# 24 of 84 weight blocks are prepared by GpSimd in the mixer of a decoder layer, and attention keeps 15 a batch

## The reference, cut to what matters

```python
# 1 mixer: project to 128 channels, two gated state-space layers over the 4 sequences' transposed axis, project back
h = gelu(x @ w_down.T + b_down); h = hydra(hydra(h)); x = norm(x + x_init + (gates of h and xmid) @ w_up.T + b_up)
# 2 cross attention over 1601 context rows, 16 heads, latent width 64
x = norm(x + softmax(q @ C_kv.T / 8) @ C_kv @ Wv)
# 3 feed forward of width 3584 with weights in integers (0 to 15), a zero and a scale for each 128 rows
w = (w_int - zero) * scale
x = norm(x + (silu(x @ gate) * (x @ up)) @ down)
```

## Time and profile before

| | us |
|---|---|
| median of 3 runs | 2754.25 (2748.42 to 2755.49) |
| the profiled execution's own time | 2750.6 |
| its span, first to last instruction | 2748.8 |
| TensorE busy | 2612.6 |
| VectorE busy | 2315.1 |
| GpSimd busy | 1956.5 |

### The profile page before, as it was taken

One profiled execution on the slowest core, in us unless ns is written; L12 is line 12 of the kernel. 1 busy time (PEld: TensorE's weight loads), 2 busy tenths in 40 slices (PEclk: granted clock), 3 DMA queues, 4 the chain that ended last, 5 costly groups with the idle time before them and its releaser, 6 DMA issues.

```text
span 2748.8 us, 41969 instructions
## 1 busy us (share of the span) xinstructions
PE 2612.6 (95%) x14328; PEld 1986.5 (72%) x14328; DVE 2315.1 (84%) x2664; ACT 1678.0 (61%) x2628; POOL 1956.5 (71%) x1431
## 2 busy tenths in 40 slices
...
GB/s 275 177 92 206 230 224 220 192 241 204 214 203 257 220 205 194 263 226 215 194 278 65 92 102 91 71 76 70 70 69 131 77 85 77 70 115 78 83 94 77
DMA packets 166791, 420.63 MB, mean 153 GB/s; under 512 B 30130, under 2 KB 57652, under 8 KB 166068
## 3 DMA queue, kind: packets, MB, share of 16 engines
...
...
## 4 chain that ended last, share of the span: by engine, by line
PE 51%; DVE 4%; SPq 3%; ACT 3%; issue 2%; POOL 1%; DMA 1%; ACTq 0%; POOLq 0%; DVEq 0%
PE c_ps L1570 42%; PE b_po L1035 4%; PE b_sc L1016 3%; SPq L909 3%; ACT b_pr L1098 1%; PE b_mi L1045 1%; PE b_mi L1054 1%; DVE b_nm_first L1178 1%; DVE c_sum_g L1726 1%; PE c_ps L1582 0%; DVE b_pr L1189 0%; DVE b_tn L1196 0%; DVE c_stats L1786 0%; DMA wint_g<-b_rw 0%; ACT b_pt L1113 0%
## 5 line engine op out<-in xcount | busy, mean ns | idle before, releaser
L1726 DVE SCALAR_TENSOR_TENSOR c_acc<-c_ps,c_sd,c_acc 128x1024 f32<-128x1024 f32 x440 | 562.9, 1282 | 90.9 <-PE c_ps L1570 90.9
L1628 ACT ACTIVATE c_scaled<-c_ps,c_sgu 128x1024 f32<-128x1024 f32 x336 | 375.2, 1117 | 423.5 <-PE c_ps L1570 417.3
L1098 ACT ACTIVATE b_pr<-b_sc,b_nm 128x799 f32<-128x799 f32 (+1 forms) x512 | 477.1, 933 | 165.4 <-DVE b_pr L1189 145.1
L1811 POOL TENSOR_TENSOR c_sum_u<-c_sum_u,c_scaled 128x1024 f32<-128x1024 f32 x168 | 404.5, 2408 | 100.8 <-ACT c_scaled L1628 99.2
L1811 POOL TENSOR_TENSOR c_sum_g<-c_sum_g,c_scaled 128x1024 f32<-128x1024 f32 x168 | 404.8, 2410 | 74.0 <-ACT c_scaled L1628 72.9
L1016 PE MATMUL b_sc<-b_kh,b_qs 128*128 128x402 f32 (+1 forms) x1024 | 399.8, 390 | 48.9 <-ACT b_pr L1098 45.2
L1297 POOL COPY b_pt<-b_tn 32x640 f32<-32x640 f32 x430 | 306.9, 714 | 155.0 <-DVE b_tn L1196 97.1
L1196 DVE STREAM_TRANSPOSE b_tn<-b_pr 128x1280 f32<-128x1280 f32 x256 | 385.6, 1506 | 24.6 <-DMA b_pt<-b_tn 9.8
L1016 PE MATMUL b_sc<-b_kl,b_qs 128*128 128x402 f32 (+1 forms) x1024 | 356.7, 348 | 0.0
L1726 DVE SCALAR_TENSOR_TENSOR c_sum_g<-c_ps,c_sgu,c_sum_g 128x1024 f32<-128x1024 f32 x224 | 286.4, 1279 | 26.2 <-PE c_ps L1570 20.8
L1189 DVE TENSOR_SCALAR_CACHE_REDUCE b_pr<-b_sc,b_nm_first 128x799 f32<-128x799 f32 x256 | 268.8, 1050 | 38.3 <-PE b_sc L1016 13.7
(11 more groups left out here) (203 smaller groups left out, 4718.7 us busy)
## 6 DMA issues: line engine op xcount, KB each, us to landing
...
c_uw_int<-wint_u SPq DMA_DIRECT2D x56, 512.0 KB, 3.5
c_gw_int<-wint_g SPq DMA_DIRECT2D x56, 512.0 KB, 3.4
c_dw_int<-wint_d SPq DMA_DIRECT2D x56, 512.0 KB, 3.5
a_cx<-in_b_ctxT SPq DMA_DIRECT2D x16, 1608.0 KB, 9.9
b_rw<-in_c_gw SPq DMA_DIRECT2D x28, 512.0 KB, 4.3
b_rz<-in_c_gz SPq DMA_DIRECT2D x28, 512.0 KB, 5.5
```

The source lines that it names most:

```text
L1098: S.activation(pr[u % 2][:, k0:k1], sc[:, at + lo:at + hi], ACT.Exp, bias=nm[:, u % 2:u % 2 + 1], accum_out=den[:, g % 2, q, half:half + 1 ...
L1628: S.activation(dst[:, :], pair[SLOT[x, t] % 4][:, :], ACT.Identity, scale=scale(x, t)).then_inc(s_e, 1)
L1726: V.scalar_tensor_tensor(out=total, in0=pair[SLOT[x, t] % 4][:, :], scalar=scale(x, t), in1=before, op0=ALU.mult, op1=ALU.add).then_inc(s_ ...
L1811: G.tensor_tensor(total, total, scaled[m % 2][:, :], ALU.add).then_inc(s_add, 1)
```

## The change

GpSimd prepares the first 24 blocks in the mixer. It waits for the second of the four input projections, then loads, subtracts, casts and stores block after block, two loads ahead, with all three kinds of DMA issued from its own queue, into buffers laid over `xt[:, 1]` and `cq`. Behind the 24 blocks it waits for their stores, and only then comes to the bias adds of L764, which before came at once. Attention prepares the other 60 blocks, 15 a batch, at the pairs of a new list `BUSY`. Several semaphores of the mixer are merged so that there are enough (`first` into `xin[0]`, `s_xmid` into `s_prep`, `s_gates` into `s_soft`, and others), with the waits' counts raised to match; the order of the work in these places is the same. Those hunks are left out here.

```diff
--- before.py
+++ after.py
@@ -34,6 +34,7 @@
 PAIR_BANK = (1, 4, 5, 4, 1, 4, 5, 4)
 CX_EARLY = {7: 0, 11: 1}
 AHEAD = 4
+EARLY_BLOCKS = 24
 TURNED_IN_GATES = 2
 SQUARES_AT = 12
 
@@ -49,6 +50,10 @@
 HEADS = 16
 
 
+NBLK = INTER // P
+BLOCKS = [(n, j) for j in range(NBLK) for n in "gud"]
+
+
 def key_tiles(kv, t):
     if t >= NDT:
         return [(slice(0, P), kv[0:LAT, t * P:(t + 1) * P])]
...
@@ -152,6 +158,10 @@
 
         def quarter(l):
             return xt[:, l, :, :] if l < 2 else late_x[:, l - 2, :, :]
+        spare = xt[:, 1, :, :].rearrange("p c n -> p (c n)")
+        rw = [spare[:, j * HID:(j + 1) * HID].bitcast(I32) for j in range(2)]
+        rw += [cq[:, j * HID:(j + 1) * HID].bitcast(I32) for j in range(2)]
+        rz = [spare[:, j * HID:(j + 1) * HID].bitcast(I32) for j in range(2, 4)]
         later = sp[:, 0:2, :, :, :].rearrange("p a l b k -> p (a l b k)").rearrange("p (b t s h) -> p b t s h", b=QT, t=L, s=L)
         flat = lambda a: a.rearrange("p l b h -> p (l b h)")
         X, (E, U1, R, M) = flat(dt[:, :, :, :]), [flat(sp[:, k, :, :, :]) for k in range(4)]
...
@@ -219,12 +229,11 @@
                 Q.wait_ge(stored[r], NT // RING * 16)
             for k in range(2):
                 Q.wait_ge(s_kvout[k], 4 * 4 * 16)
-            Q.wait_ge(s_early, 32)
+            Q.wait_ge(s_wts, 64)
 
         def tensor():
-            T.wait_ge(first, 32)
             for l in range(L):
-                T.wait_ge(xin[l + 1 if l else 0], 16)
+                T.wait_ge(xin[l + 1 if l else 0], 16 if l else 48)
                 for c in range(KC):
                     if l == 0 and c == 4:
                         T.wait_ge(xin[1], 16)
...
@@ -528,6 +536,9 @@
                 r = t % RING
                 if t >= RING:
                     S.wait_ge(stored[r], 16 * (t // RING))
+                if t == 0:
+                    for k in range(2):
+                        S.wait_ge(s_wout[k], 16 * EARLY_BLOCKS // 2)
                 S.wait_ge(s_nmr, t + 1)
                 S.activation(xo[:, r, :], xr[:, r, :], ACT.Identity, bias=nmr[:, r:r + 1], scale=rstd[:, r:r + 1]).then_inc(s_out, 1)
                 S.wait_ge(s_out, t + 1)
...
@@ -751,11 +762,40 @@
             normalise(NT - 1)
 
         def gpsimd():
-            G.wait_ge(s_prep, 3)
+            def load(i):
+                n, j = BLOCKS[i]
+                if i >= 4:
+                    G.wait_ge(s_wout[i % 2], 16 * (i // 2 - 1))
+                G.dma_start(rw[i % 4], raw[n + "w"][j, :, :]).then_inc(s_rin[i % 2], 16)
+                if i >= 2:
+                    G.wait_ge(s_sub_cast, 2 * (i - 1) - 1)
+                G.dma_start(rz[i % 2], raw[n + "z"][j:j + 1, :].broadcast_to([P, HID])).then_inc(s_rin[i % 2], 16)
+
+            def prepare(i):
+                n, j = BLOCKS[i]
+                G.wait_ge(s_rin[i % 2], 32 * (i // 2 + 1))
+                G.tensor_tensor(rw[i % 4], rw[i % 4], rz[i % 2], ALU.subtract).then_inc(s_sub_cast, 1)
+                G.wait_ge(s_sub_cast, 2 * i + 1)
+                G.tensor_copy(rw[i % 4].bitcast(F32R), rw[i % 4]).then_inc(s_sub_cast, 1)
+                if i >= 2:
+                    G.wait_ge(s_wout[i % 2], 16 * (i // 2))
+                G.wait_ge(s_sub_cast, 2 * i + 2)
+                G.dma_start(wint[n][j, :, :], rw[i % 4].bitcast(F32)).then_inc(s_wout[i % 2], 16)
+
+            G.wait_ge(s_down, 2)
+            for i in range(2):
+                load(i)
+            for i in range(EARLY_BLOCKS):
+                prepare(i)
+                if i + 2 < EARLY_BLOCKS:
+                    load(i + 2)
+            for k in range(2):
+                G.wait_ge(s_wout[k], 16 * EARLY_BLOCKS // 2)
+            G.wait_ge(s_prep, 7)
             def first_weights():
                 G.wait_ge(s_mix, 1)
                 G.memset(keys["kv"][:, NKV:KPAD], 0.0).then_inc(s_pad, 1)
-                G.wait_ge(s_early, 32)
+                G.wait_ge(s_wts, 64)
 
             for t in range(NT):
                 if t == KEYS_AT:
@@ -783,12 +823,9 @@
 SIDE = [(110, 912, 0, 802), (114, 913, 802, NKV)]
 CN_AT = {28: (1, 0), 36: (1, 1), 76: (2, 0), 84: (2, 1), 140: (3, 0), 148: (3, 1)}
 KEYS_LOAD = {24: 2, 52: 3}
-NBLK = INTER // P
-BLOCKS = [(n, j) for j in range(NBLK) for n in "gud"]
-PER_BATCH = len(BLOCKS) // L
-FREE = (2, 5, 8, 11, 14, 20, 21, 22, 23, 30, 31)
+PER_BATCH = (len(BLOCKS) - EARLY_BLOCKS) // L
 LATE = 3 * (PAIRS // L)
-BUSY = [n for n in range(PAIRS // L) if n not in FREE]
+BUSY = (0, 3, 5, 7, 8, 9, 11, 13, 15, 17, 19, 24, 26, 28, 29)
 LN_SLOTS = [15, 16, 19, 20, 23, 24, 27, 28]
 LN_VAR, LN_FACTORS, LN_PAIR, STORE_PAIR = 31, 35, 20, 23
 WEIGH_AT = 6
@@ -910,7 +947,7 @@
                                 tn[s][32 * a:32 * a + 32, c, :, :].rearrange("p t e -> p (t e)")).then_inc(s_move[s], 16)
 
             def load(i):
-                n, j = BLOCKS[i]
+                n, j = BLOCKS[EARLY_BLOCKS + i]
                 if i >= 2:
                     Q.wait_ge(s_wout[i % 2], 16 * (i // 2))
                 Q.dma_start(rw[i % 2][:, :], raw[n + "w"][j, :, :]).then_inc(s_rin[i % 2], 16)
@@ -952,7 +989,7 @@
                     store(block_of(p - 1))
                 exchange(p)
                 i = block_of(p)
-                if i is not None and i + 1 < len(BLOCKS):
+                if i is not None and EARLY_BLOCKS + i + 1 < len(BLOCKS):
                     load(i + 1)
                 if p in KEYS_LOAD:
                     Q.wait_ge(s_kl, KEYS_LOAD[p] - 1)
@@ -1512,7 +1549,7 @@
                     load_rows(0, n - (PAIRS // L - QT))
                 if p == PAIRS - 1:
                     for k in range(2):
-                        Q.wait_ge(b['wout'][k], 16 * len(BLOCKS) // 2)
+                        Q.wait_ge(b['wout'][k], 16 * (len(BLOCKS) - EARLY_BLOCKS) // 2)
                     for t in range(QT, HT):
                         load_rows(0, t)
                     Q.wait_ge(b['q'], NHEAD // 2)
```

More of the change, by code:

```diff
@@ L66, in keys_of, with mixer @@
     return out
-def mixer(nc, d, ctxT, wkv_in, wqd_in, wqk_in, wv_in, kvd, cq, ident, shared, x1):
+def mixer(nc, d, ctxT, wkv_in, wqd_in, wqk_in, wv_in, kvd, cq, ident, shared, raw, wint, x1):
     with ExitStack() as ctx:
@@ L78, in mixer @@
         T, V, S, G, Q = nc.tensor, nc.vector, nc.scalar, nc.gpsimd, nc.sync
-        first, small, small_late = sem("first"), sem("small"), sem("small_late")
+        small, small_late = sem("small"), sem("small_late")
         xin = [sem(f"xin{k}") for k in range(L + 1)]
         xres, stored = [sem(f"xres{k}") for k in range(RING)], [sem(f"out{k}") for k in range(RING)]
-        s_down, s_gelu, s_xmid = sem("down"), sem("gelu"), sem("xmid")
-        s_gates, s_prep = sem("gates"), sem("prep")
+        s_down, s_gelu = sem("down"), sem("gelu")
+        s_prep = sem("prep")
         s_z, s_sz, s_dt = sem("z"), sem("sz"), sem("dt")
-        s_soft, s_e1, s_decay_in = sem("softplus_decay"), sem("e1"), sem("decay_in")
+        s_soft, s_soft_in = sem("softplus_decay"), sem("softplus_decay_in")
         s_x, s_xc, s_tr, s_xst, s_fcd = (sem(n) for n in ("x", "xc", "tr", "xst", "fcd"))
@@ L92, in mixer @@
         s_mix, s_bup, s_up, s_res, s_var, s_std, s_nmr, s_out = (sem(n) for n in ("mix", "bup_in", "up", "res", "var", "std", "nmr", "normalised"))
-        s_wctx, s_cin, s_cmm, s_cev = sem("wkv"), [sem(f"cin{k}") for k in range(CXR)], sem("ctx_mm"), sem("ctx_evicted")
+        s_wts, s_cin, s_cmm, s_cev = sem("attention_weights"), [sem(f"cin{k}") for k in range(CXR)], sem("ctx_mm"), sem("ctx_evicted")
         s_back, s_xT, s_lat, s_cq = (sem(n) for n in ("back", "xT", "latent", "cq"))
         s_kvout = [sem(f"kv_out{k}") for k in range(2)]
-        s_early, s_kin, s_pad, s_cnp, s_cn = (sem(n) for n in ("early", "keys_in", "pad", "cn_ps", "cn"))
+        s_rin, s_sub_cast, s_wout = [sem("raw0"), sem("raw1")], sem("sub_cast"), [sem("wint0"), sem("wint1")]
+        s_kin, s_pad, s_cnp, s_cn = (sem(n) for n in ("keys_in", "pad", "cn_ps", "cn"))
         wd = sb("a_wd", [P, KC, DM])
@@ L166, in sync @@
             for dst, src in ((wd, d["wd"]), (bd, d["bd"])):
-                Q.dma_start(dst[:], src).then_inc(first, 16)
+                Q.dma_start(dst[:], src).then_inc(xin[0], 16)
             for z in range(2):
@@ L186, in sync @@
                 residual(t)
-            Q.dma_start(wkv[:, :, :], wkv_in[:, :, 0:LAT]).then_inc(s_wctx, 16)
-            Q.dma_start(wqd[:, :, :], wqd_in).then_inc(s_wctx, 16)
+            Q.dma_start(wkv[:, :, :], wkv_in[:, :, 0:LAT]).then_inc(s_wts, 16)
+            Q.dma_start(wqd[:, :, :], wqd_in).then_inc(s_wts, 16)
             def store_context(pair):
@@ L305, in project_out @@
                 elif n == 0:
-                    T.wait_ge(s_prep, 3)
+                    T.wait_ge(s_prep, 7)
                 for c in range(2):
@@ L317, in tensor @@
                 if i == 0:
-                    T.wait_ge(s_prep, 2)
+                    T.wait_ge(s_prep, 4)
                     T.wait_ge(s_gelu, L)
```

(19 more changed lines are left out.)

22 lines of the change are left out of this document (11 added, 11 removed).

## The result

The changed kernel takes 2772.6 us (median of 4 runs, 2769.7 to 2775.9) against 2754.2 for the kernel before (4 runs, 2748.4 to 2755.5): 1.0057 times as long [1.0039, 1.0076], 18.4 us slower. I had forecast 2800 us, 46 slower; the measured time lies near the low end of my 2765 to 2850, and just under the main line's own 2775 to 2835. The profiled executions took 2771.0 and 2750.6 us, with spans of 2769.2 and 2748.8: 20.4 us to explain.

A forecast was written before the change was run, and what follows sets the result against it. The prediction took VectorE's two long stretches of products to set the mixer's end. Mixer +48, DMAs +6 and attention -8 gave +46 us on the 2754.25 median, so 2800 us, with 2765 to 2850 for 8 in 10.

The forecast's parts named there:

- main line: Whole kernel: mixer +48, DMAs +6, attention -8, so +46 us to 2800; own range 2775 to 2835, chance 0.68.
- Rivals 1 and 3: Mixer: 1, long products do not wait for GpSimd, 2740 us, chance 0.10; 3, only short instructions wait, 2753, 0.07.
- rival 2: Mixer: GpSimd ends late, 12 us a block and not 8, first bias add at 315 us; about 2826 us, chance 0.15.
- +55 - 7 = +48: Mixer: VectorE delayed 55 us by GpSimd's blocks and bias adds, less 7 us regained in the first softplus chain.
- the +6 for DMAs: Mixer: early blocks' transfers cost +2 us at the start and +2 for each layer's tail; range 0 to +20.
- The price of a block: Mixer: each block's subtraction and cast, 3.41 us of GpSimd, delays VectorE in full where it is the bound.
- What the delay gives back: Mixer: nothing given back; the first stretch's +34 us passes on whole, with +3 in the second softplus chain.
- my two ways to the delay: Mixer: GpSimd's work spread evenly over the mixer gave 55 us; blocks placed one by one at 8 us each gave +56.
- The start of the mixer: Before the first stretch: -7 us from bias adds leaving the softplus chain, +3 for one block there, +2 for DMAs.
- The DMAs of the layers' tails: Mixer, end of each layer: early blocks' transfers cost +2 us for each layer's tail.
- a ceiling of 17 us: Attention's batch ends: at most 17 us to gain where the SP queue is full; half taken, -8, range 0 to -17.
- The tail: Feed-forward part after attention: same data, last block stored at the same pair, so 0.

The follow-up runs named there:

- e1: Changed kernel without GpSimd's subtraction and cast of the 24 early blocks, all their DMAs kept; 2773.9 us, 1.007.
- e2: Kernel before plus 24 subtractions and casts on scratch data in the mixer, ahead of the bias adds, no DMA added; 2790.8 us, 1.0124.
- e10: Changed kernel with five memsets of 0.95 us each in place of each early block's subtraction and cast, DMAs kept; 2749.2 us, 0.9982.
- e7: Kernel before with late bias adds, plus three subtractions and casts on scratch at the start of each layer's stretch of products; 2757.0 us, 1.0001.
- e8: Kernel before with late bias adds, plus three subtractions and casts on scratch behind each layer's second reciprocal; 2748.7 us, 0.9971.
- e3: Changed kernel without its 24 early blocks, attention keeping the thinner list of 60, feed-forward reading other blocks instead; 2739.7 us, 0.9943.
- e4: Kernel before with one added wait, putting the four first bias adds behind the first layer's projection; 2746.3 us, 0.9963.
- e9: Changed kernel with the zero blocks loaded only for the first two early blocks, arithmetic kept; 2766.1 us, 1.0043.
- e5: Kernel before with another list of free pairs, still 21 blocks a batch but none at pairs 27 to 31; 2744.8 us, 0.9958.

## Why the prediction was wrong in size

The direction and the mechanism were right: VectorE's long products do wait for GpSimd's instructions that read SBUF, shown by the rows above, by e1 (DMAs without arithmetic: no long product), e2 (arithmetic without DMAs: long products) and e10 (a busy GpSimd that reads nothing: none). Rivals 1 and 3 fell on that; rival 2 too, since the bias adds start at 208.7 us and are done well ahead of the first residual (270.6), and a block takes 7.4 us (24 of them from 27 to 204 us; I had 8). The distribution was right as well: I had put 6 blocks ahead of the first stretch, 10 into it, 6 into the gap, the last two and the adds into the second; the trace has 7, 10, 6 and 2 (one is counted on both sides of an edge). The step that failed is the mixer's "+55 - 7 = +48", with the +6 for DMAs 54, where the trace has 35.3:

- **The price of a block.** I laid its whole 3.41 us of GpSimd over VectorE's time. Measured are 2.76: 2.04 of the subtraction's 2.37 and 0.72 of the cast's 1.04. The shortfall stood in my own: L622 and L624 lost 2.04 us each, beside adds of 9.26 / 4 = 2.32. That makes the first stretch +25.8 and not +34, and the second +13.0 and not the 7 + 9 = 16 that I had for its two blocks and four adds (four adds at 2.04 are 8.2, two blocks 5.5). Together 11.2 us of the error.
- **What the delay gives back.** I let the whole delay of a stretch through, and 3 us in the gap on top. The gap got 5.7 us shorter. That my two ways to the delay agreed (55 and 56) checked neither point, since both had the 3.41 us and gave nothing back. VectorE's timeline of after, at the last square root of the first layer, has 2.10 us of idle time where 9.48 were; e7 and e8 show this by itself (8.3 us between the same work early and late). This is 8.7 us of the error and was to be seen in the profile of before: the wait stands in the timeline ahead of L701, and VectorE is busy only 6.46 of 35 us there.

```profile
149.79 1.22 DVE L707 TENSOR_TENSOR shared<-shared 128x1024 f32<-128x1024 f32 x1
153.12 0.18 DVE L712 RECIPROCAL a_rs<-a_rs 128x4 f32<-128x4 f32 x1 [2.10 <-ACT a_rs L467]
```

- **The start of the mixer.** I had -7 from the freed softplus chain, +3 for a block in it, +2 for DMAs; measured is +2.9. Of the delay here, 3.4 us lie ahead of the chain of the earlier trace rows, which starts at 60.00 us and not 56.56, with the input projections' end at 43.3 us and not 39.9; e3, without any early block, has 60.63 and 44.0, so I do not put this to the blocks. From the chain's start to the first product it is 20.2 us before, 11.8 in e4, where the adds are out of the way, and 19.7 here. So the 8.4 us that can be had there are nearly all lost again. An early block lies on the chain's later part (L639), and TensorE, which makes what the first product needs, waits 7.4 us for a tile of weights while the DMA engines are full (no such wait before). VectorE's timeline of after, and TensorE's wait:

```profile
60.00 1.27 DVE L628 TENSOR_SCALAR a_sp<-a_sp 128x128 f32<-128x128 f32 x1 [1.01 <-ACT a_sp L443]
61.73 0.64 DVE L631 TENSOR_SCALAR a_sp<-a_sp 128x128 f32<-128x128 f32 x1 [0.45 <-ACT a_sp L445]
62.41 0.23 DVE L633 TENSOR_SCALAR a_sp<-a_sp 128x128 f32<-128x128 f32 x1
62.67 0.29 DVE L635 TENSOR_TENSOR a_sp<-a_sp 128x128 f32<-128x128 f32 x1
...
64.07 2.93 DVE L639 TENSOR_TENSOR a_sp<-a_sp 128x128 f32<-128x128 f32 x1
```

```profile
PE a_ps L268 <- DMA a_wqd<-in_b_wqd: 7.4, 1, 7.4
```

- **The DMAs of the layers' tails.** I had +4. The trace has nothing that stands out (the gap's balance is the wait above; the last part is -0.7, where the thirteen profiles scatter from 107.3 to 117.1 us). Not because DMAs are cheap here: alone they cost 34 us at e1's pace and 10 at e10's. I added terms that hit the same stage; while the products are late, the context tiles arrive. That this cover is the longer stretch together with the slower pace of the blocks is argued from e1, e2 and e10; how it divides between the two was not separated.

- **Attention.** I took half of a ceiling of 17 us, -8; the trace has -11.1. The transposes of after, nine a window, answer to the earlier trace rows: 33.0 us in the steady part, as predicted, then the ends of the second and the third batch, 34.0 and 34.5 where 38.5 and 40.1 were. The sum of the excess at the first three batch ends went from 13.6 to 2.5 us, which is the whole gain:

```profile
L1233 DVE STREAM_TRANSPOSE b_tn<-b_pr x9: 1502/1505/1512, 526.2 to 559.3; 128x1280 f32<-128x1280 f32 x9
...
L1233 DVE STREAM_TRANSPOSE b_tn<-b_pr x9: 1502/1507/1511, 866.1 to 900.2; 128x1280 f32<-128x1280 f32 x9
...
L1233 DVE STREAM_TRANSPOSE b_tn<-b_pr x9: 1502/1505/1512, 1139.8 to 1174.3; 128x1280 f32<-128x1280 f32 x9
```

The profile of before was moreover one of its better ones: in the four kernels of e2, e4, e7 and e8, whose attention is unchanged, it takes 1093.6 to 1098.5 us from first to last transpose, and in e1, e3, e9 and e10, which have the new list, 1073.7 to 1080.2. That fits e3's -16.3, near my ceiling. Half of it was the wrong choice. I had counted the issues and found a quarter fewer; but what the SP queue is late by carries over to the next pair. This reading is argued from the two timelines and fits e5; no run moved one pair alone. Before, pairs 58 to 61 each had a block, and the queue issued from 802.3 to 840.6 us without a break. After, pair 59 has none, and behind its row transfer the queue stands idle for 1.1 us, from 854.85 to 855.92, ahead of pair 60's exchanges (timeline of the SP queue, after):

```profile
846.79 7.43 SPq L946 DMA_DIRECT2D b_pt<-b_tn  x9
854.27 0.58 SPq L970 DMA_DIRECT2D x<-b_y  x1
855.92 5.57 SPq L946 DMA_DIRECT2D b_pt<-b_tn  x9
861.54 0.58 SPq L953 DMA_DIRECT2D b_rw<-in_c_uw  x1
```

e5 reaches nearly the same ends (33.0, 34.4 and 35.1 us) by moving blocks away, without any early block, and pays with other places.

- **The tail.** -3.9 us after the last transpose, predicted as 0. Over all thirteen profiles this part lies between 1325.5 and 1332.5 us whatever the change, so I read it as scatter.

Of the 25.6 us between 46 and 20.4, the mixer makes 18.7, attention 3.1 and the tail 3.9.

The Trainium skill (SBUF — State Buffer, Who interferes with whom) has whoever issues first hold the shared ports for its whole instruction, with the other blocked meanwhile. The measured 2.04 of 2.37 us and 0.72 of 1.04 agree with the exclusion, and the memsets of e10, which read nothing and left the products at 1.22 us, with the kind of GpSimd instruction that it holds for. But what a product loses is 0.32 or 0.33 us less than the whole instruction; no run here says why.
